# A four-slot weight ring with a split refill wait in the gated mixtures of a vision tower

## The chip, the cores and the metric

The kernel runs on one core of one Trainium2 chip. The metric is the device time of one execution in microseconds (us), the median of several executions. Engines are named as the profile names them: PE is TensorE (PEld its weight loads), DVE is VectorE, ACT is ScalarE, POOL is GpSimd, SP is SyncE, which here only issues DMAs. All arrays are float32 unless said otherwise.

## The reference, cut to what matters

A tower of eight sections on h of shape (8 images, 257 tokens, 256 features), each section adding to h. Two of its sections are gated mixtures of experts, run over all 2056 tokens; `x` is the layer-normed h.

```python
# first mixture: 8 experts, 2 per token, hidden size 512
xn = rms_norm(x, norm_scale)
scores_topk, idx = top_k(xn @ w_router.T, 2);  weights = softmax(scores_topk)
u, gate = split(xn @ w_up[e].T, 2)             # for each chosen expert e, w_up[e]: 1024 x 256
y = (u * silu(gate)) @ w_down[e].T             # w_down[e]: 256 x 512
h = h + x + sum(weights * y)
# second mixture: 16 experts, 1 per token, hidden 512, plus one shared expert for all tokens
scores = sigmoid(logits) of the chosen expert, which scales its input
h = h + (up * silu(gate)) @ down_proj[e] + silu(x @ w_gate.T) * (x @ w_up.T) @ w_down.T
```

## The kernel before

`section_sparse` is one function for three mixtures: two gated ones (`glu` true: `moe0` with 8 experts and 2 per token, `moe1` with 16 experts, 1 per token and a shared expert) and a last one with 32 small experts (`glu` false), which this change leaves as it is. Tokens are sorted by expert into blocks of 128 rows, each block with one expert: `NBLK` = 40 blocks in the first gated mixture, 31 in the second, 71 in all. The sorted token rows are gathered from DRAM by indirect DMA from POOL (`fetch`, ring `xr` of XR = 4), and each block's result is scattered back by another (`send`, ring `yo` of YR = 3).

The weights of block b go to slot `b % WR` of two rings, `up` (8 KB in each partition and slot, 1 MB a load) and `down` (4 KB, 512 KB a load). With `WR` = 3 there are three slots. SP issues these loads in order, two for each block (`load_weights`, L2174 to L2183): it waits until the narrowing products of block b-3 are done (semaphore `y_ps`, L2177), reads the block's expert from `eb`, and issues `up` (L2182) and `down` (L2183), both counted on the slot's one semaphore `wsem[v]`. In the second mixture the shared expert's weights lie in the last slot, `WR - 1`, so the load for block `WR - 1` also waits for `sh_out`, the end of the shared expert's products (L2179, L2180). Behind the loads, on the same queue, SP waits for all scatters and loads the results `yg` back.

On PE one iteration b of the loop at the end of its program runs, in this order: `widen(b, 1)`, the gate half of the widening products of block b (L2343, 128x512 outputs, 2 products, each in two passes), `turn_hidden(b-1)`, four transposes of the hidden rows of block b-1 (L2353), `widen(b, 0)`, the other half, `turn_rows(b+1)`, two transposes of the next block's tokens (L2332), and `narrow(b-1)`, the narrowing products of block b-1 (L2362, 4 products in two passes, 8 in the trace). `widen(b, 1)` waits once for `wsem` at 32 a round, that is, for both halves of the weights. Semaphore `up_done` rises by 1 at the end of each widening half, `y_ps` at the end of each narrowing. ACT computes SiLU of the gate half and copies tokens and results out of PSUM, DVE multiplies and copies the hidden rows.

Of the kernel before, what the change touches and what calls it, by code (L numbers as in the profile page):

```python
# [45 lines left out]
def signal(nc, ctx, name):  # L46

    return ctx.enter_context(nc.semaphore(name))
# [46 lines left out]
def clear_stale(eng, k):  # L95

    for sem in k.stale:
        eng.sem_clear(sem)
# [1952 lines left out]
def chunk_width(m):  # L2051
    return min(P, NTOK - m * P)
# [10 lines left out]
def section_sparse(nc, k, tag, E, top, w_router, w_up, w_down, b_router=None, scale=None, shared=False, ahead=0):  # L2063
# [7 lines left out]
    glu = top != "one"  # L2071
    NBLK = (K * NTOK + E * (P - 1)) // P
    HID = 512
    J = HID // P
    WR, XR, YR, GR = (3, 4, 3, 6) if glu else (6, 6, 4, 6)
    NR = K * NCK
    ROWS = NCK * P
    XB = 1 if glu else 2
# [2 lines left out]
    with ExitStack() as ctx:  # L2081
# [48 lines left out]
        s = {n: signal(nc, k.sems, tag + "_" + n) for n in names}  # L2130
# [28 lines left out]
        with nc.Block() as block:  # L2159
            @block.sync  # L2160
            def _(sp):
                sp.dma_start(w_r[:], w_router).then_inc(s["r_in"], 16)
                sp.dma_start(iota[:], k.iota.partition_broadcast(P)).then_inc(s["r_in"], 16)
                sp.dma_start(tri_f[:], k.tri).then_inc(s["r_in"], 16)
                if rms:
                    sp.dma_start(sc[:], scale).then_inc(s["r_in"], 16)
                if top == "one":
                    sp.dma_start(rb[:], b_router.partition_broadcast(P)).then_inc(s["r_in"], 16)
                if shared:
                    sp.dma_start(up[:, WR - 1], w_up[E]).then_inc(s["s_in"], 16)  # L2170
                    sp.dma_start(down[:, WR - 1], w_down[E]).then_inc(s["s_in"], 16)
                clear_stale(sp, k)

                def load_weights(b):  # L2174
                    v = b % WR
                    if b >= WR:
                        sp.wait_ge(s["y_ps"], b - WR + 1)  # L2177
                    if shared and b == WR - 1:
                        sp.wait_ge(s["sh_out"], B)  # L2179
                    e = sp.value_load(eb[0:1, b:b + 1], min_val=0, max_val=E - 1)  # L2180
                    if glu:
                        sp.dma_start(up[:, v], w_up[bass.ds(e, 1)].rearrange("o p c f -> p (o c) f")).then_inc(wsem[v], 16)  # L2182
                        sp.dma_start(down[:, v], w_down[bass.ds(e, 1)].rearrange("o p c f -> p (o c) f")).then_inc(wsem[v], 16)  # L2183
                    else:
                        sp.dma_start(wt[:, v], w_up[bass.ds(e, 1)].rearrange("o p f -> p (o f)")).then_inc(wsem[v], 16)

                for m in range(NCK):
                    w = chunk_width(m)
                    sp.wait_ge(s["tok_set"], m + 1)
                    sp.dma_start(x_dram[m * P:m * P + w], tok[0:w, m, rows]).then_inc(s["x_out"], 16)  # L2190
                sp.wait_ge(s["routed"], 1)
                for b in range(NBLK):
                    load_weights(b)

                for v in range(YR):
                    sp.wait_ge(ysem[v], 16 * len(range(v, NBLK, YR)))
                for m in range(NCK):
                    w = chunk_width(m)
                    if m >= GR:
                        sp.wait_ge(s["mixed"], m - GR + 1)  # L2200
                    sp.dma_start(yg[0:w, m % GR], y_back[m * P:m * P + w]).then_inc(gsem[m % GR], 16)
# [509 lines left out]
def build(nc, a, out, last):  # L2711
    with ExitStack() as ctx:
# [20 lines left out]
        if last >= 2:  # L2733
            section_sparse(nc, k, "moe0", 8, "softmax2", a["moe0_r"], a["moe0_up"], a["moe0_down"], scale=a["moe0_scale"], ahead=B - 2)
# [4 lines left out]
        if last >= 4:  # L2739
            section_sparse(nc, k, "moe1", 16, "sigmoid1", a["moe1_r"], a["moe1_up"], a["moe1_down"], shared=True, ahead=B - 2)  # L2740
# [8 lines left out]
        if last >= 8:  # L2749
            section_sparse(nc, k, "sw", 32, "one", a["sw_wr"], a["sw_w"], None, b_router=a["sw_br"])  # L2750
# [154 lines left out]
```

## Time and profile before

| | us |
|---|---|
| median of 3 runs | 4349.88 |
| lowest and highest of the 3 | 4332.42, 4360.74 |
| the profiled execution, its time | 4347.72 |
| the profiled execution, span of its trace | 4345.6 |
| PE busy in it | 3598.7 (83%) |
| DVE, ACT, POOL busy | 2666.3, 2071.4, 1925.0 |
| mean granted TensorE clock, as a share of 2.4 GHz | 0.933 |

All times of rows are us from the start of the span. The page's strips show each engine in 40 equal slices of 108.6 us; a digit is the busy share in tenths. In a group or timeline row, "idle before" is the time in which the engine stood ahead of the instruction, with what ended it; "issue" is a release that the profile can't name. Ends of matmuls are modelled, and a following instruction may start up to 0.2 us ahead of a printed end. The first mixture's block loop lies at about 256 to 536 us, the second's at 1188 to 1400 us.

### The profile page before, as it was taken

The page shows a single profiled execution, that of the slowest core. Times are in us where ns is not written, and L with a number is a line of the kernel's source. Part 1 is how long each engine was busy: PE and PEld are TensorE (multiplying, and loading weights), DVE is VectorE, ACT ScalarE, POOL GpSimd, SP SyncE. Part 2 cuts the span into 40 slices and gives each one's busy share as a digit, 9 for nine tenths or more (in the row PEclk, how much of TensorE's full clock was granted, in tenths as well). Part 3 has the DMA queues.
Part 4 walks back from the last instruction along what each step waited for, and adds up shares of the span by engine and source line. Part 5 has one row for each costly group of instructions (what it writes and reads, how often), then busy time and mean ns, then how long its engine had stood idle before and what let it go on. Part 6 is the DMA issues. An engine that isn't in the chain of part 4 may idle for free. (4 is left out here: it accounts for less than half of the span.)

```text
span 4345.6 us, 61242 instructions
## 1 busy us (share of the span) xinstructions
PE 3598.7 (83%) x19616; PEld 2465.4 (57%) x19616; DVE 2666.3 (61%) x3928; ACT 2071.4 (48%) x4736; POOL 1925.0 (44%) x1894
## 2 busy tenths in 40 slices
PE   2868878898888788888888888888887788888867
PEld 1545475565654456666666666666655555555544
DVE  6432124444222699999999999999994333333331
ACT  1321112223111677777777777777762243334321
POOL 0122200000022499898999999898982000000034
PEclk9889969999999799999999999999999999999965
DMA  3057620000176100000000000000000000000035
GB/s 89 2 207 270 227 73 1 1 1 28 59 257 230 33 1 1 2 1 2 1 13 1 3 1 1 2 1 2 1 1 10 25 1 1 1 1 1 3 106 152
DMA packets 66640, 196.96 MB, mean 45 GB/s; under 512 B 12704, under 2 KB 37401, under 8 KB 55993
## 3 DMA queue, kind: packets, MB, share of 16 engines
q1 hardware_dynamic: 54968, 161.81, 11.2%
q0 software_dynamic: 11328, 30.95, 2.3%
q8 instruction: 170, 2.79, 0.3%
q14 instruction: 174, 1.42, 0.1%
HBM read 166.74 MB, written 25.99 MB: 44 GB/s over the span
## 5 line engine op out<-in xcount | busy, mean ns | idle before, releaser
L1876 DVE TENSOR_TENSOR_SCAN ssm_hs<-ssm_da,ssm_pb 128x512 f32<-128x512 f32 x1024 | 1240.4, 1211 | 3.6 <-ACT ssm_da L1715 3.6
L1415 POOL TENSOR_TENSOR ssm_hc<-ssm_hs,ssm_cb 128x1024 f32<-128x1024 f32 x512 | 1207.3, 2358 | 0.0
L1512 PE MATMUL ssm_py<-ssm_hc,ident 128*128 128x256 f32 x4096 | 1059.1, 381 | 3.7 <-POOL ssm_hc L1415 3.7
L1715 ACT ACTIVATE ssm_da<-ssm_dt,ssm_an 128x255 f32<-128x255 f32 x2048 | 871.5, 502 | 132.0 <-POOL ssm_dtu L1363 88.4
L1512 PEld LDWEIGHTS ssm_py<-ssm_hc,ident 128*128 128x128 f32 x4096 | 704.6, 191 | 79.0 <-POOL ssm_hc L1415 5.4
L1859 DVE TENSOR_TENSOR ssm_pb<-ssm_pb,ssm_dtu 128x512 f32<-128x512 f32 x1024 | 694.2, 678 | 26.2 <-PE ssm_pb L1498 24.0
L1498 PE MATMUL ssm_pb<-ssm_bst,ssm_eyeb 96*128 96x256 bf16 x2048 | 403.5, 279 | 210.5 <-DVE ssm_hs L1876 195.2
L1498 PEld LDWEIGHTS ssm_pb<-ssm_bst,ssm_eyeb 96*128 96x128 bf16 x2048 | 147.2, 98 | 488.0 <-DVE ssm_hs L1876 413.8
L1114 DVE TENSOR_REDUCE duo_mxr<-duo_ring 128x4 f32<-128x1024 f32 x128 | 156.6, 1224 | 315.9 <-PE duo_ring L847 304.9
L2343 PE MATMUL moe_pu<-moe_up,moe_xt 128*128 128x512 f32 x568 | 275.0, 607 | 59.7 <-issue 57.6
L2215 POOL DMA_INDIRECT moe_xr<-moe_x_dram,moe_rowx x71 | 68.7, 967 | 428.7 <-PE ln_ps L2332 267.0
L2675 DVE COPY moe_ht<-moe_pz 128x512 f32<-128x512 f32 x71 | 49.1, 692 | 305.2 <-PE moe_pz L2353 305.2
L1748 ACT COPY ssm_cb<-ln_ps 128x256 f32<-128x256 f32 x512 | 165.9, 379 | 72.2 <-PE ln_ps L1484 71.5
L747 POOL TENSOR_TENSOR duo_qb<-duo_bm,duo_q 128x4 f32<-128x4 f32 x32 | 6.3, 196 | 424.8 <-ACT duo_k L989 424.8
L747 POOL TENSOR_TENSOR lat_qb<-lat_bm,lat_q 128x4 f32<-128x4 f32 x32 | 6.3, 198 | 414.8 <-DVE lat_k L1102 414.8
L2343 PEld LDWEIGHTS moe_pu<-moe_up,moe_xt 128*128 128x128 f32 x568 | 98.3, 192 | 153.9 <-issue 150.6
L841 PE MATMUL duo_ring<-duo_k,duo_q 32*128 32x256 f32 x1024 | 147.0, 405 | 45.3 <-DVE duo_mxr L1114 45.0
L1005 ACT ACTIVATE duo_ex<-duo_ring 128x1024 f32<-128x1024 f32 x128 | 130.8, 1023 | 103.5 <-PE duo_ring L847 103.5
L1414 POOL COPY ssm_hl<-ssm_hs 128x4 f32<-128x4 f32 x512 | 96.7, 189 | 149.9 <-DVE ssm_hs L1876 63.5
L841 PEld LDWEIGHTS duo_ring<-duo_k,duo_q 32*128 32x128 f32 x1024 | 94.2, 189 | 101.6 <-issue 47.8
L847 PE MATMUL duo_ring<-duo_q,duo_k 32*128 32x256 f32 x1024 | 146.7, 406 | 0.0
L1463 PE MATMUL ln_ps<-xb,ssm_win 128*128 128x257 f32 x512 | 134.5, 387 | 4.5 <-POOL xb L1324 2.6
(590 smaller groups left out, 6069.7 us busy)
## 6 DMA issues: line engine op xcount, KB each, us to landing
moe_up<-in_moe_up SPq DMA_DIRECT2D x72, 1024.0 KB, 5.4
moe_down<-in_moe_down SPq DMA_DIRECT2D x72, 512.0 KB, 6.2
sw_wt<-in_sw_w SPq DMA_DIRECT2D x47, 192.5 KB
moe_x_dram<-moe_tok SPq DMA_DIRECT2D x32, 128.0 KB
moe_yg<-moe_y_dram SPq DMA_DIRECT2D x16, 256.0 KB
tok_w<-in_wd SPq DMA_DIRECT2D x4, 576.0 KB, 13.0
out<-h SPq DMA_DIRECT2D x1, 2056.0 KB, 7.4
tok_pix<-in_img SPq DMA_DIRECT2D x1, 2048.0 KB, 9.7
```

The lines of the kernel that those rows point to most:

```text
L841: ins1 = nc.tensor.matmul(dst1[:, o, at:at + w], q[r, b1, t * P:t * P + P], kk[r, b1, a, 0:w], start=not causal, stop=not causal or t == 1)
L847: ins2 = nc.tensor.matmul(dst2[:, o, at:at + 256 - q0], kk[r, b2, a, t * P:t * P + P], q[r, b2, q0:256], start=not causal, stop=not causal ...
L1114: ins = nc.vector.tensor_reduce(mxr[:, a, js, :], src.rearrange("p o (t s) -> p o t s", t=2), AX, ALU.max)
L1415: nc.gpsimd.tensor_tensor(hc[:, n % 2, part_], hs[:, n % 2, part_], cb[:, q * NQ_ + 4 * half:q * NQ_ + 4 * half + 4, :], ALU.mult).then_in ...
L1463: ins = nc.tensor.matmul(pm[:, n % 2, 0:T], w_in[:, c, n * P:n * P + P], k.xb[:, c, 0:T], start=(c == 0), stop=(c == C - 1))
L1498: ins = nc.tensor.matmul(pb[:, p % 4, o, :], one_state(st), bst2[:, v, 0:L], start=True, stop=True)
L1512: ins = nc.tensor.matmul(py[:, j % 2, 0:L], k.ident[:], hc[:, n % 2, st, :], start=False, stop=(q == QN - 1 and st == NQ_ - 1))
L1715: ins = nc.scalar.activation(da[:, n % 2, 2 * m + o, 1:L], dt2[:, v, j, 1:L], ACT.Exp, scale=a_n[:, d, j, st:st + 1])
L1748: nc.scalar.copy(cb[:, st, :], pm[:, st % 2, 0:L]).then_inc(s["c_free"], 1)
L1859: nc.vector.tensor_tensor(b2, b2, dtu2[:, v, j:j + 1, 0:L].broadcast_to([P, 2, L]), ALU.mult).then_inc(s["b_set"], 1)
L1876: nc.vector.tensor_tensor_scan(two(hs[:, n % 2, 2 * m:2 * m + 2, :]), two(da[:, n % 2, 2 * m:2 * m + 2, :]), two(pb[:, p % 4]), 0.0, ALU.m ...
L2343: ins = nc.tensor.matmul(pu[:, b % 2, g, :], xt[:, b % 2, c, :], up[:, b % WR, c, g * HID:g * HID + HID], start=(c == 0), stop=(c == C - 1))
```

## The change

The ring of the gated mixtures has four slots instead of three. A load of the `up` half into a slot in use now waits for `up_done` at 2 x (b - 3), that is, until both widening halves of block b-4 are done. Between the issue of the `up` half and that of the `down` half SP waits for `y_ps` at b - 3, the narrowing products of block b-4. The shared expert's slot, `WR - 1`, becomes slot 3, and with it the block whose load waits for `sh_out` becomes block 3. The last mixture's waits are unchanged.

```diff
@@ -2072,7 +2072,7 @@
     NBLK = (K * NTOK + E * (P - 1)) // P
     HID = 512
     J = HID // P
-    WR, XR, YR, GR = (3, 4, 3, 6) if glu else (6, 6, 4, 6)
+    WR, XR, YR, GR = (4, 4, 3, 6) if glu else (6, 6, 4, 6)
     NR = K * NCK
     ROWS = NCK * P
     XB = 1 if glu else 2
@@ -2174,12 +2174,14 @@
                 def load_weights(b):
                     v = b % WR
                     if b >= WR:
-                        sp.wait_ge(s["y_ps"], b - WR + 1)
+                        sp.wait_ge(s["up_done"] if glu else s["y_ps"], (2 if glu else 1) * (b - WR + 1))
                     if shared and b == WR - 1:
                         sp.wait_ge(s["sh_out"], B)
                     e = sp.value_load(eb[0:1, b:b + 1], min_val=0, max_val=E - 1)
                     if glu:
                         sp.dma_start(up[:, v], w_up[bass.ds(e, 1)].rearrange("o p c f -> p (o c) f")).then_inc(wsem[v], 16)
+                        if b >= WR:
+                            sp.wait_ge(s["y_ps"], b - WR + 1)
                         sp.dma_start(down[:, v], w_down[bass.ds(e, 1)].rearrange("o p c f -> p (o c) f")).then_inc(wsem[v], 16)
                     else:
                         sp.dma_start(wt[:, v], w_up[bass.ds(e, 1)].rearrange("o p f -> p (o f)")).then_inc(wsem[v], 16)
```

## Rows read from the trace of the kernel before

**Rows 1.** The page: busy us of the engines, and the strips of 40 slices.

```profile
PE 3598.7 (83%) x19616; PEld 2465.4 (57%) x19616; DVE 2666.3 (61%) x3928; ACT 2071.4 (48%) x4736; POOL 1925.0 (44%) x1894
...
PE   2868878898888788888888888888887788888867
...
DMA  3057620000176100000000000000000000000035
```

**Rows 2.** The page's groups: count, then busy us, mean ns, idle before and releaser.

```profile
L2343 PE MATMUL moe_pu<-moe_up,moe_xt 128*128 128x512 f32 x568 | 275.0, 607 | 59.7 <-issue 57.6
```

**Rows 3.** Windows over both loops, block 2 to last: length, busy us by engine.

```profile
core 0: us, PE busy (x) PEld busy (x) DVE busy (x) ACT busy (x) POOL busy (x), PEclk, DMA share, GB/s
268.41:526.65 258.24, 224.79 (x816) 131.18 (x814) 51.19 (x74) 50.42 (x112) 69.14 (x71) 0.99 0.75 262
1198.62:1392.20 193.58, 169.18 (x617) 98.50 (x616) 38.74 (x56) 38.15 (x85) 50.89 (x52) 1.00 0.76 264
```

**Rows 4.** Timeline (start us, us, engine): first and last of the 67 blocks in those windows.

```profile
268.41 1.88 PE L2343 MATMUL moe_pu<-moe_up,moe_xt 128*128 128x512 f32 x4
...
1385.60 0.34 SPq L2182 DMA_DIRECT2D moe_up<-in_moe_up  x1
...
1392.20 1.96 PE L2343 MATMUL moe_pu<-moe_up,moe_xt 128*128 128x512 f32 x4 [0.31 <-issue]
```

**Rows 5.** Timeline of one block: narrowing, the two loads, the next two widenings.

```profile
404.33 1.89 PE L2362 MATMUL ln_ps<-moe_down,moe_ht 128*128 128x256 f32 x8
...
406.97 0.34 SPq L2182 DMA_DIRECT2D moe_up<-in_moe_up  x1
...
407.02 1.95 PE L2343 MATMUL moe_pu<-moe_up,moe_xt 128*128 128x512 f32 x4 [0.80 <-issue]
407.49 0.33 SPq L2183 DMA_DIRECT2D moe_down<-in_moe_down  x1
...
413.88 1.96 PE L2343 MATMUL moe_pu<-moe_up,moe_xt 128*128 128x512 f32 x4 [0.80 <-issue]
```

**Rows 6.** Timeline: a long load, and a block that starts without a stall.

```profile
275.15 0.34 SPq L2182 DMA_DIRECT2D moe_up<-in_moe_up  x1
...
283.67 1.96 PE L2343 MATMUL moe_pu<-moe_up,moe_xt 128*128 128x512 f32 x4 [1.67 <-issue]
285.46 0.60 PE L2353 MATMUL moe_pz<-ident,moe_hid 128*128 128x128 f32 x4
...
289.57 1.88 PE L2343 MATMUL moe_pu<-moe_up,moe_xt 128*128 128x512 f32 x4
291.28 0.60 PE L2353 MATMUL moe_pz<-ident,moe_hid 128*128 128x128 f32 x4
...
297.37 1.96 PE L2343 MATMUL moe_pu<-moe_up,moe_xt 128*128 128x512 f32 x4 [1.82 <-issue]
```

**Rows 7.** Timeline of a stalled widening, and a window behind it (columns of rows 3).

```profile
497.94 2.66 PE L2343 MATMUL moe_pu<-moe_up,moe_xt 128*128 128x512 f32 x4 [2.21 <-issue]
...
500.00:502.00 2.00, 2.00 (x6) 1.19 (x5) 0.51 (x1) 0.60 (x1) 0.00 (x0) 0.50 0.97 391
```

**Rows 8.** A window over the first three loads, and the first gather (timeline).

```profile
241.00:252.00 11.00, 3.58 (x34) 3.33 (x34) 6.95 (x11) 0.44 (x2) 0.07 (x1) 0.60 0.99 409
...
251.93 1.12 POOL L2215 DMA_INDIRECT moe_xr<-moe_x_dram,moe_rowx  x1 [30.40 <-DVE moe_rowx L2649]
...
255.04 0.66 PE L2332 MATMUL ln_ps<-ident,moe_xr 128*128 128x128 f32 x2 [5.19 <-DMA moe_xr<-moe_x_dram,moe_rowx]
```

**Rows 9.** Timeline at the start of the second mixture's loop.

```profile
1187.37 0.34 SPq L2182 DMA_DIRECT2D moe_up<-in_moe_up  x1
...
1198.62 1.88 PE L2343 MATMUL moe_pu<-moe_up,moe_xt 128*128 128x512 f32 x4
...
1206.89 1.95 PE L2343 MATMUL moe_pu<-moe_up,moe_xt 128*128 128x512 f32 x4 [2.29 <-issue]
```

**Rows 10.** The gathered tokens' tile: who waited for it (us, times).

```profile
PE ln_ps L2332: 5.2, 1
```

**Rows 11.** A window of dense PE work in the second mixture (columns of rows 3).

```profile
1140.00:1180.00 40.00, 39.72 (x193) 33.56 (x192) 10.21 (x26) 5.78 (x15) 3.85 (x4) 1.00 0.05 14
```

**Rows 12.** A window just behind a landing in the loop (columns of rows 3).

```profile
414.00:414.50 0.50, 0.50 (x2) 0.26 (x3) 0.00 (x0) 0.00 (x0) 0.50 (x1) 1.00 0.00 0
```

## Prediction, written before the changed kernel was seen

> **What bounds the kernel now.** I read the page first. One core, TensorE (PE) busy 83% of the span, and two stretches where the DMA digits stand at 5 to 7 while PE stands at 6 to 8 (third to fifth and 12th to 13th digit): the two gated mixtures [rows 1]. L2343, the widening product, idled 59.7 us ahead of itself, 57.6 of it released by "issue", that is, by nothing that this profile can name [rows 2]. The code has three waits there: for the copied tokens, for the multiplied hidden rows of two blocks before, and for the weights. The first two come from ACT and DVE, which the profile names as releasers elsewhere; what is left is the landing of the weights.
>
> Then the stretches. From the first widening product of block 2 to that of the last block the first mixture takes 526.65 - 268.41 = 258.24 us for 37 blocks, the second 1392.20 - 1198.62 = 193.58 us for 28: 451.82 us for 65 blocks, 6.95 us each, moving 262 and 264 GB/s [rows 3, 4]. PE is the only engine near its limit; ACT is busy 50.42 us and DVE 51.19 us of 258.
>
> One block, in order of time, shows the loop. The narrowing products start at 404.33 and PE is idle until 407.02 with 0.80 us of it marked "issue", so they ended at 406.22. SP then issues the two halves of block 23's weights, at 406.97 and 407.49. Block 23's widening starts at 413.88, 6.91 us behind the first issue. In between PE did block 22 (407.02 on) and stood 0.80 us [rows 5]. So the cycle is: narrowing done, 0.75 us to the issue, about 6.9 us to the landing of both halves, widening. With three slots a load has one iteration of PE, about 6 us, to hide behind. From issue to widening it takes 6.9 us here, 8.52 us in the longest of the stalled blocks (275.15 to 283.67), and 6.60 us for the last one (1385.60 to 1392.20), one of the shortest [rows 4 to 6]. Where a load comes a little early the next widening starts at once, and the stall is paid by the block after it: 283.67 (1.67 idle), 289.57 (none), 297.37 (1.82) [rows 6].
>
> The same rows give PE's own pace. The hidden transposes of two consecutive blocks, with no stall between them, start at 285.46 and 291.28: **5.82 us** per block [rows 6]. Nothing but the weights makes it longer: in iterations such as 289.57 PE waits for no other engine.
>
> **The change, part by part.** *A fourth slot.* It adds 12 KB to each partition and no instruction. A load for block b now waits for block b-4. Its narrowing ends at the end of iteration b-3, so both halves have two iterations of PE ahead of them instead of one: 2 x 5.82 = 11.6 us, less 0.75 us to the issue, against 8.5 us for the longest load. The stall goes.
>
> *The split wait.* up(b) waits for the widening of block b-4, down(b) for its narrowing. SP is one queue, in order: behind down(b) stands up(b+1), whose widening (block b-3, in iteration b-3) is over some 2 us before narrowing b-4 releases SP. So from the second refill on, down(b) and up(b+1) go out as a pair, 0.5 us apart, at the end of iteration b-3. The widening half gains an iteration of lead, but not "as soon as" in the literal sense. Its consumer waits for both halves, so down(b) is what counts, and it is now first of the pair. What stands behind the new wait on SP is only the next loads; after the loop come the waits for the y stores, and the last of these loads is out three iterations earlier. The extra wait costs SP nothing that PE sees: it issues two DMAs in 6 us.
>
> *The sum.* 65 blocks at 5.82 instead of 6.95 us: 451.82 - 378.3 = **73.5 us**. In that is the one block that ran partly at the lower clock (from 497.94 on: its first half takes 2.66 us instead of 1.96). The granted clock was 0.50 there, the lower level of 1.2 GHz, behind a 2.21 us stall of PE [rows 7]; without the stall I expect none of it. Blocks 0 to 2 keep their pace: they were loaded ahead before, too.
>
> *What else moves.* (a) Block 3 of the first mixture is now loaded ahead, right behind 0 to 2. The three loads, 4.72 MB, nearly fill the window from 241 to 252, which moved 4.5 MB at 409 GB/s and a DMA share of 0.99; a fourth, 1.57 MB at that rate, keeps the engines busy 3.8 us more, to about 256. The first gather of tokens is issued at 251.93 and PE waits for it until 255.04 [rows 8]. It must share now. Bound below: 0. Bound above: the whole 3.8 us. In the loop the gathers share the engines with the loads, and no other gather was waited for [rows 10], so I take 1 us, near the lower end. (b) In the second mixture the shared expert sits in the last slot, now slot 3: block 2 no longer waits for it (its load went out at 1187.37 and it started at 1198.62 without a stall, so 0), and block 3 goes out there instead, which removes the 2.29 us stall at 1206.89 that is in the sum [rows 9]. (c) The gathers are issued four blocks ahead and the stores of y have three slots. PE waited for a gather once in 71, those 5.2 us at the start [rows 10], so the cover is about 20 us against a queue that now runs fuller; 0 to 1 us, I take 1. (d) PE runs denser. Does its clock hold? It did at 39.72 busy us of 40, at 1.00 [rows 11]: 0.
>
> 73.5 - 2 = 71.5 us. The profiled execution (4347.7 us, span 4345.6) lies 2.2 us below the median of the three runs, 4349.9; the sum is a difference, so it goes on the median: **4278 us**.
>
> **The next limit, and the rivals.** *Rival A: the DMA engines become the bound.* A block moves 1.57 MB of weights, 0.13 MB of gathered and 0.13 MB of stored rows. In the loop the mean share of the 16 engines is 0.75 and 0.76: 0.75 x 258.24 / 37 = 5.2 us of transfer per block, 90% of 5.82 [rows 3]. Against the rival: back to back, three loads ran at 409 GB/s, which would make 4.5 us of it [rows 8], and in the loop the share falls to 0.00 behind a landing [rows 12]. For it: 90% is a mean over the 16 engines, and would hide one that is slower. The Trainium skill, page "DMA: Bandwidth & Descriptors", section "Latency and other measured facts", says that DMA engines 7 and 15 are usually slower than the rest; no row here splits the engines, so nothing here shows it. If the slowest lies over 12% above the mean, it sets the pace, from 5.9 us on up to 6.6 us, a short issue-to-start of a pair with no overlap of pairs at all [rows 4]. The saving is then 65 x 1.05 = 68 down to 65 x 0.35 = 23 us: 4282 to 4327, middle 4305.
>
> *Rival B, slower: two pairs in flight slow each other beyond the old period.* Its place is the same queue: if every pair took the longest time seen, 8.5 us, with no overlap, 65 x (8.5 - 6.95) = 101 us come on top: 4451 [rows 6]. It decides from 6.95 us per block on. Against it stand the three pairs that went in 11 us of transfer, 3.7 us each [rows 8].
>
> *Rival C: the change doesn't do what it says.* The early refill of the widening half is undone by SP's order, as above, so only the slot counts. That changes no number of mine, since the slot alone gives two iterations of cover. It would matter only if the fourth slot could not be kept filled, which is A.
>
> *Rival D: the time is given back elsewhere.* What follows both loops is unchanged and starts earlier. But stretches outside run at either clock level; 20 us of PE work at 1.2 instead of 2.4 GHz costs 10. The three runs span 28 us. It shifts the result by some 10 us either way.
>
> **How the numbers follow.** PE-bound at about 5.8 us, 4278: 0.72, its own range 4264 to 4290 by the spread of the runs. A: 0.20, of which about a third ends above 4306. D with a shift over 15 us: 0.04, half of it each way. B: 0.04. One per cent, 43.5 us, is about what a measurement of this kernel can tell from no change, so the edges are 4306 and 4393. Faster by over 1%: nearly all of the first, two thirds of A and half of D, 0.71 + 0.13 + 0.02 = 0.86. Within 1%: the rest of A and of D, 0.10. Slower: B, 0.04. The range takes in the first case and two thirds of A or more: 4262 to 4312.
>
> **What would show it.** In the changed profile: the wait of L2343 on "issue" falls from 57.6 to under 10 us (block 0 of each mixture has a little). Each loop's blocks come 5.8 us apart, and the loops last about 215 and 163 us from block 2 to the last. GB/s there rises to 310 or so and the DMA share to 0.85 to 0.9; GpSimd's and ACT's busy times stay. SP issues moe_down, then moe_up 0.5 us behind it, the reverse of now. A is seen as periods above 5.9 with stalls on "issue" while the DMA share is near 1; if the share instead stays at 0.75 with stalls, SP's order is at fault and my account of the queue is wrong. A new wait of PE on moe_xr or of ACT on the y stores would show (c) mispriced. The prediction fails if the period stays above 6.3 us, or if PE's granted clock in the loops drops below 0.98.

## The result

| | before | after |
|---|---|---|
| median, us | 4343.8 (4 runs: 4332.42 to 4360.74) | 4277.91 (4 runs: 4260.94 to 4294.31) |
| ratio | | 0.984, 95% interval 0.9807 to 0.9873 |
| span of the profiled execution | 4345.6 | 4292.3 |
| both loops, block 2 to last | 258.24 + 193.58 | 215.34 + 162.96 |
| L2343 (after: L2345) idle ahead, "issue" | 57.6 | 0 |

Faster by 1.6%, with 4278 us predicted. By the ratio that is 69.5 us of 4343.8, interval 55 to 84; 71.5 us were forecast. That the median met the forecast to 0.1 us is luck: the single runs lie 33 us apart, and the forecast started from a median of before of 4349.9 us, which a fourth run moved to 4343.8. What the trace shows of the loops is not luck, and it is sharper than the median.

The group of the widening products, from the page of the changed kernel, against [rows 2]:

```profile
L2345 PE MATMUL moe_pu<-moe_up,moe_xt 128*128 128x512 f32 x568 | 269.6, 598 | 1.8 <-ACT moe_xt L2471 1.8
```

The 1.8 us left are waits for the copied tokens of the first blocks. The windows over both loops, columns as in [rows 3], first block 2 to the last of either mixture:

```profile
287.75:503.09 215.34, 215.34 (x815) 133.31 (x814) 51.17 (x74) 50.08 (x111) 68.70 (x70) 1.00 0.85 302
1177.54:1340.50 162.96, 162.96 (x618) 100.86 (x617) 38.72 (x56) 37.93 (x84) 51.04 (x52) 1.00 0.84 298
```

PE is busy in all of both stretches, 37 and 28 blocks at 215.34/37 = 162.96/28 = 5.82 us, at a DMA share of 0.84 and 0.85 (forecast: 0.85 to 0.9) and some 300 GB/s (forecast: 310). Both means include the last blocks, whose loads are already out; from 300 to 480 us the share was 0.89 at 316 GB/s. ACT, DVE and POOL do the same work as before in less time. One block in order of time, the timeline of the changed kernel, to be held against [rows 5]:

```profile
340.13 1.88 PE L2345 MATMUL moe_pu<-moe_up,moe_xt 128*128 128x512 f32 x4
...
340.47 0.33 SPq L2185 DMA_DIRECT2D moe_down<-in_moe_down  x1
...
341.57 0.34 SPq L2182 DMA_DIRECT2D moe_up<-in_moe_up  x1
...
345.95 1.88 PE L2345 MATMUL moe_pu<-moe_up,moe_xt 128*128 128x512 f32 x4
...
346.29 0.33 SPq L2185 DMA_DIRECT2D moe_down<-in_moe_down  x1
```

The down half goes out first, then the up half of the next block, 1.1 us behind it, and no widening product has idle time ahead of it any more.

The spans differ by 53.3 us though, not by the 73.5 us of the loops. Cut at the same events, the two profiles give:

| stretch, by its last event | before | after | difference |
|---|---|---|---|
| start to the first load of the first mixture (SP, L2162) | 179.49 | 195.34 | +15.9 |
| to the first stores of tokens (L2190, after: L2192) | 50.46 | 50.98 | +0.5 |
| to block 0 of the first mixture | 26.21 | 28.65 | +2.4 |
| blocks 0 to 2 | 12.25 | 12.78 | +0.5 |
| block 2 to the last | 258.24 | 215.34 | -42.9 |
| to block 0 of the second mixture | 661.66 | 664.14 | +2.5 |
| block 0 to 2 | 10.31 | 10.31 | 0.0 |
| block 2 to the last | 193.58 | 162.96 | -30.6 |
| to the end | 2953.4 | 2951.8 | -1.6 |

The largest thing that is not the loops is the first row, in a section that the change doesn't touch. The windows show its cause. First the kernel before, then the changed one; columns as in [rows 3]:

```profile
120.00:152.00 32.00, 32.00 (x103) 21.90 (x102) 6.76 (x17) 6.00 (x18) 1.97 (x8) 0.50 0.00 1
156.00:176.00 20.00, 20.00 (x116) 14.63 (x116) 6.88 (x19) 6.46 (x20) 2.15 (x8) 1.00 0.00 1
```

```profile
120.00:184.00 64.00, 64.00 (x204) 43.64 (x202) 12.15 (x31) 12.03 (x36) 3.25 (x12) 0.50 0.00 1
```

The granted clock fell to 0.50 (1.2 GHz) at about 120 us in the kernel before and 117 us in the changed one, and stayed there for 34 and 72 us. Per us PE got through 103/32 = 3.2 matmuls at 0.50 and 116/20 = 5.8 at 1.00. The +2.5 us between the mixtures are clock too: PE ran the same products there (3753 and 3754 in the trace) with the same idle time (102.8 and 102.9 us), but was busy 561.3 instead of 558.9 us at a mean clock of 0.91 instead of 0.92. Two questions were open: which part of the change makes the gain, and whether the change has a hand in that low clock.

### The profile page after: what moved, and what is told of

Read it like the earlier page. It is cut to its first block and busy times, and to the rows that moved or that the text cites. A ratio compares the mean times of both kernels' runs of the same rounds, so it can differ in the third digit from the quotient of the medians.

```text
span 4292.3 us, 61244 instructions
## 1 busy us (share of the span) xinstructions
PE 3605.7 (84%) x19616; PEld 2486.0 (58%) x19616; DVE 2666.0 (62%) x3928; ACT 2072.7 (48%) x4736; POOL 1927.1 (45%) x1894
## 5 line engine op out<-in xcount | busy, mean ns | idle before, releaser
L2345 PE MATMUL moe_pu<-moe_up,moe_xt 128*128 128x512 f32 x568 | 269.6, 598 | 1.8 <-ACT moe_xt L2471 1.8
L1748 ACT COPY ssm_cb<-ln_ps 128x256 f32<-128x256 f32 x512 | 166.2, 380 | 70.4 <-PE ln_ps L1484 69.9
L2345 PEld LDWEIGHTS moe_pu<-moe_up,moe_xt 128*128 128x128 f32 x568 | 103.1, 192 | 76.8 <-issue 70.4
```

Source lines behind the costliest of these rows:

```text
L1748: nc.scalar.copy(cb[:, st, :], pm[:, st % 2, 0:L]).then_inc(s["c_free"], 1)
L2345: ins = nc.tensor.matmul(pu[:, b % 2, g, :], xt[:, b % 2, c, :], up[:, b % WR, c, g * HID:g * HID + HID], start=(c == 0), stop=(c == C - 1))
```

## The experiments

Every run is compared with runs of the kernel before on the same chip. "Loops" are the periods per block behind block 2, in the first and the second mixture.

### The changed kernel again

> The changed kernel itself, on the chip of the next three, as their yardstick. Its profile had all 65 blocks behind the third of each mixture 5.82 us apart, 73.5 us less than before, but a span only 53.3 us shorter, since the section ahead of the first mixture took 18.8 us longer, at a granted clock of 0.50 for longer. If that section has nothing to do with the change, its length differs again here, while the blocks stay at 5.82 us; if the change caused it, the first mixture starts near 275 us again. Expected: ratio to before 0.983, first block anywhere from 253 to 275 us.

Measured: 4255.35 us (4 runs: 4249.08 to 4270.18) against 4330.06; ratio 0.9829 (0.9788 to 0.9871). Loops 5.82 and 5.82, block 0 at 253.11 instead of 274.97. The low clock lasted 24 us this time. Chips differ: before stood at 4330 on this one, so only ratios and traces carry over.

### The slot alone

Against the changed kernel:

```diff
-                        sp.wait_ge(s["up_done"] if glu else s["y_ps"], (2 if glu else 1) * (b - WR + 1))
+                        sp.wait_ge(s["y_ps"], b - WR + 1)
...
-                        if b >= WR:
-                            sp.wait_ge(s["y_ps"], b - WR + 1)
```

> Four slots, but the old wait: both halves of a load wait for the narrowing products of the block four back. My account says that the widening half is not refilled earlier by the split wait in any way that PE can see, so this gives the whole gain: 5.82 us per block in both loops, no stall on the weights, ratio 0.983. If the early refill of the widening half carries part of the gain, stalls on the weights come back and a block takes over 5.9 us.

Measured: 4265.73 us, ratio 0.9851 (0.9803 to 0.99). Loops 5.82 and 5.82, 215.34 and 162.96 us long, the changed kernel's lengths to the hundredth, no stall on the weights. The split wait adds nothing to the fourth slot.

### The split wait alone

Against the changed kernel:

```diff
-    WR, XR, YR, GR = (4, 4, 3, 6) if glu else (6, 6, 4, 6)
+    WR, XR, YR, GR = (3, 4, 3, 6) if glu else (6, 6, 4, 6)
```

> Three slots, with the split wait. SP's order makes the queue send down(b) and then up(b+1) at the end of iteration b-2: the widening half has two iterations of lead, the narrowing half one, but as the first and smaller of the pair. By my account 512 KB at the head of the queue land in some 4 us, less than the 5.07 us that are left of an iteration, so the stall goes here too: 5.82 to 5.9 us per block, ratio 0.983 to 0.985, with 12 KB a partition less. The rival: what counts is the transfer of 1.5 MB a block and its lead of one iteration, so the stalls stay and a block takes 6.9 us, ratio 1.00.

Measured: 4275.61 us, ratio 0.9867 (0.9822 to 0.9912). Loops 5.87 and 5.90: 217.25 + 165.28 = 382.5 us, 4.2 us more than with four slots and 69.3 us less than before. So either half of the change makes nearly all of the gain by itself. The windows of this kernel:

```profile
285.90:503.15 217.25, 216.34 (x815) 133.01 (x814) 51.20 (x74) 50.04 (x111) 68.50 (x70) 1.00 0.87 307
1175.29:1340.57 165.28, 164.34 (x618) 100.26 (x617) 38.75 (x56) 37.86 (x84) 50.90 (x52) 1.00 0.86 303
```

What is left is a thin margin. The timeline of this kernel at its first stall:

```profile
292.05 0.33 SPq L2185 DMA_DIRECT2D moe_down<-in_moe_down  x1
...
298.21 1.96 PE L2345 MATMUL moe_pu<-moe_up,moe_xt 128*128 128x512 f32 x4 [0.51 <-issue]
```

The down half that block 4 needs left SP at 292.05 and the block could start 6.16 us later. A block without a stall has 5.5 us there. I had put this landing at some 4 us; the median is 4.8. The up half issued 4.7 us earlier is then still in the queue (its own landing takes 7.4 us in the median), which is the likely reason.

### Only the order of the halves

```diff
+                        sp.dma_start(down[:, v], ...).then_inc(wsem[v], 16)
                         sp.dma_start(up[:, v], ...).then_inc(wsem[v], 16)
-                        sp.dma_start(down[:, v], ...).then_inc(wsem[v], 16)
```

On three slots with the old wait.

> Three slots and the old wait, only the order of the two loads of a block turned: down first, then up. The block waits for both, so if lead is what counts nothing changes: 6.9 us per block, 55 to 60 us of stall on the weights. If it were the order of the halves in the queue that helped in the kernel with three slots and the split wait, it would show here as well, with a block under 6.5 us.

Measured, a single run: 4347.39 us. Loops 7.54 and 7.00, 69.4 us idle on "issue" ahead of the widening products. No gain, as expected: the order by itself does not help, and what the kernel with the split wait has beyond it is the lead. I had expected 6.9 us per block and 55 to 60 us of stall, though, and not a first loop 20 us longer than before. A row of it shows how:

```profile
313.58 3.65 PE L2343 MATMUL moe_pu<-moe_up,moe_xt 128*128 128x512 f32 x4 [4.03 <-issue]
```

Behind a 4.03 us stall the same four matmuls took 3.65 us instead of 1.88 to 1.96. In 10 us windows over that loop the granted clock is 0.83 to 0.95 in nine of 29. The stalls cost twice: once as idle time, once as low clock behind them. Of the 23 us that both loops together took longer than before, 11.8 are idle time. Why the stalls themselves grew is not shown; it is one profile.

### How far the DMA engines are from being the bound

```diff
+            spill = sb("spill", [P, 2, 1, 2 * HID])      # with 1 MB: 2 instead of 1
...
+                        if b >= 2:
+                            sp.wait_ge(extra_in[b % 2], 16 * (b // 2))
+                        sp.dma_start(spill[:, b % 2], w_up[...][:, 0:1]).then_inc(extra_in[b % 2], 16)
```

> The changed kernel with 512 KB more to load per block: a third DMA reads half of the same widening weights into a scratch ring of two that nothing reads. It finds how far the DMA engines are from being the bound. A block then moves 1.57 + 0.26 + 0.52 = 2.36 MB. If the rate at full share is what the loop before showed (262 GB/s at a share of 0.75, that is 350 GB/s), a block takes 6.7 us and PE stalls some 0.9 us on the weights. If the engines can do the 409 GB/s of the loads ahead of the loop, it takes 5.8 us and PE stays the bound.

> The same with 1 MB more per block, 2.88 MB in all. DMA-bound by either rate: 8.2 us per block at 350 GB/s, 7.05 us at 409 GB/s. The difference to the run with 512 KB more gives the price of 512 KB in a saturated queue, and so what a block of the changed kernel would take if PE were not in the way: 5.2 us by the first rate, 4.5 us by the second.

With 512 KB more per block: 4305.07 us (a single run, low clock for 68 us ahead of the loop); loops 5.82 and 5.82, no stall. With 1 MB more: 4341.94 us (a single run), stalls in both loops. Windows of the first kernel, then of the second:

```profile
287.76:503.10 215.34, 215.34 (x815) 133.20 (x814) 51.16 (x74) 50.08 (x111) 68.48 (x70) 1.00 0.98 390
```

```profile
340.00:500.00 160.00, 139.77 (x508) 81.11 (x507) 31.82 (x46) 31.14 (x69) 44.99 (x46) 1.00 1.02 416
```

In the second the queue is full (share 1.02) and the blocks are 6.93 us apart (from 401.29 to 435.92 for five). 2.88 MB / 6.93 us = 416 GB/s. The 1.83 MB of a block of the changed kernel would take 4.4 us at that rate: 76% of 5.82, where I had said 90%. Neither expectation's first rate (350 GB/s) was right; the second (409) was. The difference of the two runs, which I had meant to take as the price of 512 KB, gives none, since PE was still the bound in the first.

### Three slots with PE's waits apart

```diff
+        dsem = [signal(nc, k.sems, tag + "_d_in%d" % v) for v in range(WR)]
...
-                            pe.wait_ge(wsem[b % WR], (32 if glu else 16) * (b // WR + 1))
+                            pe.wait_ge(wsem[b % WR], 16 * (b // WR + 1))
...
+                        pe.wait_ge(dsem[b % WR], 16 * (b // WR + 1))    # ahead of the narrowing products
```

On three slots with the split wait; the down half counts on `dsem`.

> Three slots with the split wait, and on PE the waits apart too: each half has semaphores of its own, the widening products wait for the widening half alone and the narrowing products for the narrowing half. Three slots with the split wait alone took 5.87 and 5.90 us per block, with a few periods of 6.5 us. If what was left there was the landing of the narrowing half, one iteration behind its issue, this takes it away: 5.82 us in every block, as with four slots, and a ratio of 0.983. If it was the queue itself, a stall on the weights stays.

Measured: loops 5.82 and 5.82, 215.34 and 162.96 us, as with four slots. The window of the first:

```profile
255.31:470.65 215.34, 215.34 (x815) 133.48 (x814) 51.16 (x74) 50.03 (x111) 68.47 (x70) 1.00 0.88 309
```

So what the split wait alone left was the landing of the down half, and with both waits apart three slots do what four do. The time, 4286.85 us (4261.65 to 4296.16), ratio 0.9863 (0.9821 to 0.9904), cannot show it; the spread is the next topic.

### Where the spread comes from

In each of the eleven profiles in which nothing fills that wait, PE stands 2.03 or 2.04 us in the section ahead of the first mixture, waiting for a running sum that DVE and ACT work out, and the granted clock falls to 0.50 within 3 us behind it. The timeline of the changed kernel's second profile:

```profile
116.93 0.26 PE L443 MATMUL ln_ps<-ident,mem_cum 8*128 8x8 f32 x2 [2.04 <-issue]
...
119.81 2.32 PE L435 MATMUL mem_pk<-mem_wk,x 128*128 128x64 f32 x12
```

L435 takes 1.31 us at 1.00 and 2.32 at 0.50. How long it stays low differs: 7, 14, 17, 24, 27, 34, 34, 48, 68, 72 and 72 us in these profiles, whatever the kernel (twice the shortfall of the granted clock, summed over windows of 1 us). The fill puts four matmuls, whose result nothing reads, into the stall:

```diff
                 project(0)
                 pe.wait_ge(s["exp_gate"], 1)
+                for n in range(4):
+                    nc.tensor.matmul(p_s[:, 0:T], k.mean[:], k.x[:, n % C, 0, :], start=True, stop=True)
                 spread(0)
```

> The changed kernel with four matmuls more in the section ahead of the first mixture, whose result nothing reads: they fill the 2.04 us for which PE waits there for the gate's running sum, behind which the granted clock fell to 0.50 in all six profiles, for 14 to 68 us. If that stall brings the low clock on, the clock stays at 1.00 from 112 to 176 us, the section ends at about 162 us instead of 170 to 197, and the kernel is 10 to 30 us faster than the changed one: ratio to before 0.977, against 0.983. If the small products of that section bring it on, nothing changes: the clock falls a few us later and the ratio stays at 0.983.

Measured: 4260.88 us (6 runs: 4257.15 to 4263.91), ratio 0.9797 (0.9766 to 0.9827). The timeline of this kernel at the same place:

```profile
114.51 2.00 PE L482 MATMUL mem_ps<-x,mean 128*128 128x257 f32 x8
116.57 0.28 PE L443 MATMUL ln_ps<-ident,mem_cum 8*128 8x8 f32 x2
...
119.26 1.32 PE L435 MATMUL mem_pk<-mem_wk,x 128*128 128x64 f32 x12
...
112.00:163.00 51.00, 49.50 (x284) 35.89 (x282) 19.57 (x45) 16.11 (x50) 4.30 (x16) 1.00 0.00 1
```

L443 waits no more, L435 stays at 1.32 us, the clock stays at 1.00 (last row, a window with the columns of [rows 3]) and the first load of the first mixture leaves at 163.0 us instead of 167 to 197. The six runs lie within 6.8 us, those of before on that chip, 11 of them, over 36 us.

The control, the same four matmuls behind `spread(0)`, so that the stall stays:

> A control to the kernel with the stall filled: the same four matmuls, whose result nothing reads, but behind the products that wait for the running sum, so that the 2.04 us stall of PE stays. If it is the stall that brings the low clock on, the clock falls to 0.50 at about 118 us for 14 us or more, and the times spread like those of the changed kernel. If the mere presence of more large products keeps the clock up, the section runs at 1.00 here too and the times lie within 10 us of 4260.

Measured: 4270.23 us (4263.93 to 4280.22), ratio 0.9815 (0.9781 to 0.985). Its rows:

```profile
117.17 0.26 PE L443 MATMUL ln_ps<-ident,mem_cum 8*128 8x8 f32 x2 [2.04 <-issue]
...
117.89 2.47 PE L483 MATMUL mem_ps<-x,mean 128*128 128x257 f32 x8
...
120.00:124.00 4.00, 4.00 (x13) 2.89 (x12) 0.61 (x2) 0.00 (x0) 0.00 (x0) 0.50 0.00 0
```

The clock fell while the four extra matmuls (L483, 8 in the trace) ran, and stayed low for 17 us. The median lies 10.2 us from 4260 and its interval takes in both cases, so the time can't decide this; the trace does. With the stall the clock fell in eleven profiles of eleven, also with the extra products behind it, and with the stall filled in neither of two (the second is the kernel before with the fill, below). It is the stall that brings it on, not the size of the products in that section.

> The changed kernel once more, as the yardstick of the two kernels with fill matmuls. Its blocks are 5.82 us apart whatever happens ahead of them. If the low clock of the section ahead of the first mixture is what spreads its times, they spread over 15 to 30 us again, around a median of 4255 to 4280 us.

The changed kernel once more, on this chip: 4272.82 us (6 runs: 4264.6 to 4291.13), ratio 0.9833 (0.9803 to 0.9863), loops 5.82. Its six runs lie 26.5 us apart, against the 6.8 us of the six with the fill.

> The kernel before, three slots and the old wait, with the 2.04 us stall of the section ahead of the first mixture filled by the four matmuls. If the low clock there and the weight ring have nothing to do with each other, the times lose their spread and stand at the lower end of those of before, 4332 to 4345 us, ratio 0.995; the blocks still take 6.9 us. Against the 4260.9 us of the changed kernel with the fill, it gives the gain of the ring without that noise: I expect 73 us, the 73.5 of the blocks less 1 to 3 us for the first gather.

The kernel before with the fill: 4333.69 us (12 runs: 4322.06 to 4343.1), ratio 0.997 (0.9952 to 0.9987), so 0.3% faster than without. Its loops are 6.90 and 6.90. Against the changed kernel with the fill that is 4333.69 - 4260.88 = 72.8 us, on two chips whose medians for before differ by 0.4 us (4350.92 and 4351.28). Expected were 73. That it met them is partly luck: in the two profiles the loops differ by 448.7 - 378.3 = 70.4 us, of which the longer wait for the first gather (7.7 against 5.1 us) takes 2.6 back. Its spread is 21 us, not the 7 us of the changed kernel with the fill: my expectation that the spread would go was half wrong. Where the rest of it lies is not shown; the stalls of its loops are one candidate, since a low clock followed one of them in [rows 7], and one of 2.39 us in the profile of this kernel (0.50 around 407 us).

The changed kernel with the fill is the best version here: ratio 0.9797 against 0.984, 0.9829 and 0.9833 of the changed one. Its interval ends at 0.9827, so the lead of some 0.36% is likely rather than certain from the ratios. The traces show where it comes from: a first load at 163.0 us, against 174 to 195 in the three profiles of the changed kernel.

## Why the prediction was right, point by point

- **The bound and PE's own pace: right.** Weights landing one iteration behind their issue were the stall, and 5.82 us, read between two rows of [rows 6], is the period of all 65 blocks. The sum of 73.5 us came out as 42.90 + 30.62 = 73.5 us. The slot alone, the split wait alone and the waits apart show that the mechanism is the lead of the loads.
- **SP's order: right, one size off.** The pairs are down(b), up(b+1), 1.1 us apart and not 0.5; in the code the wait for `up_done` and the read of the block's expert lie between. It costs nothing.
- **The split wait adds nothing: right for four slots, incomplete.** I argued it only on top of the slot. On three slots it makes 69 of the 73.5 us, which I did not see when I predicted: the down half then has one iteration, but at the head of its pair. The prediction's "only the slot counts" is true of this change and false of the idea.
- **The first gather: mis-sized.** PE waited 7.6 us for it instead of 5.2: 2.4 us where I took 1. In the five other profiles with four slots and no extra load it was 7.5 to 7.9 us, in the four others with three slots 5.0 and 5.1, so it goes with the fourth load.
- **Gathers and stores in a fuller queue: 0 where I took 1.** PE waited for one gather in 71, as before; ACT for no store. The +2.5 us between the mixtures and the +0.5 us of blocks 0 to 2 (mean clock 0.80 instead of 0.84) had no term in the sum.
- **Rival A, the DMA engines: wrong in its size, rightly held the lesser.** I made 5.2 us of transfer per block from a share of 0.75. Saturated, the engines do a block in 4.4 us. The share counted more time per byte the less full the queue was: 262 GB/s at 0.75, 302 at 0.85, 390 at 0.98, 416 at 1.02 are 349, 355, 398 and 408 GB/s per full share (why is not shown). Half a megabyte more per block was free, so the chance of 0.20 was too high. The slower DMA engines that the Trainium skill speaks of (page "DMA: Bandwidth & Descriptors", section "Latency and other measured facts") did not bind: a block with 2.36 MB, 29% more than the 1.83 MB of the changed kernel, still took 5.82 us (this holds if the extra load is spread over the engines like the rest). Whether some engines are slower no view here shows.
- **Rival B: no.** No pair in flight together came too late for its block, with 0.5 MB more per block neither. Whether they slowed each other by less than that is not shown; with the split wait alone, an up half took 7.4 us to land in the median.
- **Rival D: right in kind, larger than said.** I gave 10 us either way. The section ahead of the first mixture alone moved the profiled pair by 15.9 us and can move a run by some 30 (from 167 to 197 us at its end). It isn't tied to the change: the changed kernel itself showed 24, 27 and 72 us of low clock.

## What to carry to other kernels

When PE's idle time sits ahead of one product per block and the releaser is a load, read the period that the kernel would have without it from two like instructions with no stall between them; it was exact here. A ring gains from lead, and lead can come from a slot or from splitting a wait: try the split first, as it costs no memory, and wait for each half only where it is read. Ask of every short PE stall what the clock does behind it, since a 2 us wait cost up to some 30 us here.

## What the runs showed of the hardware

- **The low clock outlasts its cause by far, and for a time that varies.** Behind one and the same 2.04 us stall the granted clock stayed at 0.50 for 7 to 72 us, in the changed kernel with PE busy in all 64 us of the window from 120 to 184. The Trainium skill, page "TensorE: Matmul & The Clock Gate", section "Part 1: The HAM clock gate (the "warmup" mystery)", says that the throttled state is the default and that activity releases it. The fall behind an idle stretch agrees with the traces; a steady stream of products that didn't release it for over 60 us is more than that sentence lets one expect. What ends the low stretch stays open. The products of that stretch of the kernel are small (8 to 64 rows or columns in many), which may matter; no run changed them.
- **A single stall of 2 us can suffice, and need not.** In the kernel before, a stall of 2.21 us in the first loop was followed by the low clock [rows 7], and one of 2.29 us in the second was not [rows 9]: the second loop ran at 1.00 throughout [rows 3].
- **One core's DMA engines held 416 GB/s** of mixed loads, gathers and stores for 160 us, in the kernel with 1 MB more per block.
